# A gated attention and sign-weight FFN block on one core: row statistics taken a batch sooner, signs taken one by one, first weights' low parts split otherwise, raw output weights in another place

## The reference

```
xn  = layernorm(x)                       # per row, eps 1e-5
q   = xn @ wq.T ; k_new = xn @ wk.T ; v_new = xn @ wv.T
k   = concat(ctx, k_new) ; v = concat(ctx, v_new)     # 1024 keys
att = softmax(q @ k.T / sqrt(512)) @ v
x   = x + tanh(g_xattn) * (att @ wo.T)
h   = relu((layernorm(x) @ sign(up).T) * up_scale)    # 2048 hidden
x   = x + tanh(g_ffn) * (h @ sign(down).T) * down_scale * output_scale
```

## Time and profile before

| | |
|---|---|
| median of 3 runs | 663.87 us (663.48 to 664.93) |
| profiled execution's own time | 664.24 us |
| its span, first to last instruction | 662.5 us |
| TensorE busy | 602.3 us (91%) |
| VectorE busy | 382.2 us (58%) |
| ScalarE busy | 290.0 us (44%) |
| GpSimd busy | 132.7 us (20%) |
| mean granted TensorE clock | 0.964 |

### The profile page before, as it was taken

One profiled execution on the slowest core, in us unless ns is written; L12 is line 12 of the kernel. 1 busy time (PEld: TensorE's weight loads), 2 busy tenths in 40 slices (PEclk: granted clock), 3 DMA queues, 4 the chain that ended last, 5 costly groups with the idle time before them and its releaser, 6 DMA issues.

```text
span 662.5 us, 7100 instructions
## 1 busy us (share of the span) xinstructions
PE 602.3 (91%) x2738; PEld 494.3 (75%) x2738; DVE 382.2 (58%) x527; ACT 290.0 (44%) x426; POOL 132.7 (20%) x116
## 2 busy tenths in 40 slices
PE   7959993999993999994999986999999999999997
PEld 6747772888872888873888865888888787888885
DVE  4498724267734248744158753965555955666564
ACT  3573601154511146521137436546565834555541
POOL 5673000202000201100200300431423201324001
PEclk9969996999997999998899997999999999999999
DMA  8603202010201104101102013220101031132011
GB/s 290 234 0 129 64 0 77 19 63 1 64 1 34 62 17 174 64 1 32 63 1 95 2 63 127 72 88 33 63 33 64 32 128 32 54 107 96 1 64 63
DMA packets 20097, 43.21 MB, mean 65 GB/s; under 512 B 4832, under 2 KB 4832, under 8 KB 19680
## 3 DMA queue, kind: packets, MB, share of 16 engines
q1 hardware_dynamic: 20064, 42.76, 19.0%
HBM read 36.45 MB, written 6.30 MB: 65 GB/s over the span
## 4 chain that ended last, share of the span: by engine, by line
PE 68%; DMA 9%; issue 8%; DVE 8%; ACT 5%; POOL 2%; SPq 0%; POOLq 0%; DVEq 0%; ACTq 0%
PE proj L527 19%; PE score L657 17%; PE turn L642 11%; PE score L527 7%; DMA row_facts<-mean_rstd 4%; PE proj L642 4%; PE score L560 4%; PE proj L560 2%; DMA all_facts<-row_facts 2%; DVE raw_t L1200 2%; DMA raw_w<-in_ffn_w 1%; POOL four_x L455 1%; PE score L788 1%; DVE turned_x L1299 1%; DVE turned_x L1302 1%
## 5 line engine op out<-in xcount | busy, mean ns | idle before, releaser
L657 PE MATMUL score<-down_signs,hid_split 128*128 128x512 f32 x512 | 133.8, 390 | 0.6 <-DVE normed L1515 0.5
L527 PE MATMUL proj<-probsT,four_x 128*128 128x512 f32 x384 | 97.7, 416 | 35.2 <-DVE four_x L1179 35.2
L527 PEld LDWEIGHTS proj<-probsT,four_x 128*128 128x128 f32 x384 | 76.8, 203 | 53.9 <-DVE four_x L1179 37.5
L657 PEld LDWEIGHTS score<-down_signs,hid_split 128*128 128x128 f32 x512 | 95.8, 188 | 21.7 <-DVE hid_split L1482 0.9
L527 PE MATMUL proj<-four_x,weights 128*128 128x512 f32 x336 | 79.2, 396 | 5.8 <-ACT raw_q L888 5.8
L455 POOL TENSOR_TENSOR four_x<-raw_ctx,four_x 128x2048 fp32r<-128x2048 f32 x8 | 37.2, 4645 | 216.5 <-ACT four_x L869 216.5
L527 PEld LDWEIGHTS proj<-four_x,weights 128*128 128x128 f32 x336 | 64.2, 192 | 19.9 <-issue 6.6
L1179 DVE TENSOR_TENSOR four_x<-proj,four_x 128x512 fp32r<-128x512 f32 x32 | 22.0, 689 | 54.4 <-ACT four_x L877 54.4
L1482 DVE TENSOR_TENSOR hid_split<-hid,hid_split 128x512 fp32r<-128x512 f32 x64 | 44.0, 690 | 15.8 <-ACT hid_split L1093 15.6
L527 PE MATMUL proj<-weights,four_x 128*128 128x512 f32 x192 | 51.9, 405 | 0.0
L642 PE MATMUL turn<-ops_b,up_ops 128*128 128x512 f32 x192 | 51.8, 391 | 0.0
(11 more groups left out here) (128 smaller groups left out, 885.9 us busy)
## 6 DMA issues: line engine op xcount, KB each, us to landing
raw_w<-in_ffn_w SPq DMA_DIRECT2D x24, 512.0 KB, 3.3
raw_ctx<-in_ctx_turned SPq DMA_DIRECT2D x4, 1024.0 KB, 5.3
raw_ctx<-in_ctx SPq DMA_DIRECT2D x4, 1024.0 KB, 5.8
result<-rows SPq DMA_DIRECT2D x16, 256.0 KB, 2.0
rows<-in_x SPq DMA_DIRECT2D x3, 1024.0 KB, 5.4
turned_x<-in_x_turned SPq DMA_DIRECT2D x3, 1024.0 KB, 5.3
rows_away<-rows SPq DMA_DIRECT2D x1, 2048.0 KB, 10.8
rows<-rows_away SPq DMA_DIRECT2D x1, 2048.0 KB, 7.6
```

Source lines behind the costliest of these rows:

```text
L527: last = pe.matmul(bank, lhs(l), rhs(r), start=start and i == 0, stop=stop and i == 2)
L657: last = pe.matmul(wide(r), hid_split[:, n % HR, s, r * P:(r + 1) * P], down_signs[:, chunk_of(q), :], start=(q == 0 and s == HI), stop=(q ...
```

## The change

- `row_facts`/`all_facts` become a function of their own, `next_facts`. In batches 1 and 2 SP calls `next_facts(b+1)` ahead of `next_rows(b+1)`, right after the raw context of batch b. Row statistics of batch b + 2 are taken by VectorE after the attention of batch b is added, ahead of the next keys, and `inverse_std(b+1)` stands ahead of the value context's low part on GpSimd. Batch 1's statistics are still taken in batch 0, after the last probabilities.
- `norm_turned` stands behind `proj_out` of e = 0 (in batch 0: behind e = 3), `next_rows_low` behind e = 1 (3), and `next_hi` on ScalarE behind e = 1 (3).
- In the start, VectorE makes the low parts of `wq` and of the first turned context; GpSimd makes those of `wk` as before, then waits for batch 0's last score operand (S4) before those of `wv`, the value context and `wo`. The high parts of `wv` and `wo` move into batch 0. `t_high(T1)` moves behind key 2. There is one `w_ready` semaphore for each matrix.
- Raw `wo` lies in `rows[8:12]`, the place of `wq` and of batch 2's `x`, and is loaded after `wq` is split; batch 2's `x` is loaded after `wo` is split.
- The first attention product waits for the new values one row tile at a time.
- In the last batch the eight sign pieces are taken at different points of ScalarE's queue instead of four in a row.

```diff
-    SPLIT = {W_K: 0, W_Q: DC, W_O: 2 * DC, W_V: 3 * DC}
+    SPLIT = {W_K: 0, W_Q: DC, W_V: 2 * DC, W_O: 3 * DC}
-                  W_O: probs[:, 0:2, :].rearrange("p s (k n) -> p (s k) n", n=DIM)}
+                  W_O: rows[:, 2 * RT:3 * RT, :]}
@@ SP
-            sp.dma_start(raw_of[W_O], wo.rearrange(row_tiles, p=P)).then_inc(w_in[W_O], 16)
...
+            sp.wait_ge(w_ready[W_Q], DC)
+            sp.dma_start(raw_of[W_O], wo.rearrange(row_tiles, p=P)).then_inc(w_in[W_O], 16)
...
+                if b == 0:
+                    sp.wait_ge(w_ready[W_V], DC)
+                    sp.dma_start(rows[:, 3 * RT:4 * RT, :], x_v[3]).then_inc(x_in[3], 16)
+                    next_rows(1)
+                    next_facts(1)
+                    sp.wait_ge(w_ready[W_O], DC)
+                    sp.dma_start(rows[:, 2 * RT:3 * RT, :], x_v[2]).then_inc(x_in[2], 16)
+                elif b + 1 < BATCH:
+                    next_facts(b + 1)
+                    next_rows(b + 1)
@@ GpSimd
             weight_low(W_K, 3)
-            for i in range(DC):
-                weight_low(W_Q, i)
-            context_low(turned_split(0))
-            for i in range(DC):
-                weight_low(W_O, i)
-            for i in range(DC):
-                weight_low(W_V, i)
             for b in range(BATCH):
+                if b == 0:
+                    pool.wait_ge(s_ready, nth(S_LO, 0, S4))
+                    for i in range(DC):
+                        weight_low(W_V, i)
+                else:
+                    inverse_std(b + 1)
                 context_low(values_split(b))
-                inverse_std(b + 1)
+                if b == 0:
+                    for i in range(DC):
+                        weight_low(W_O, i)
+                    inverse_std(1)
@@ TensorE
-                pe.wait_ge(proj_lo, values_out(b, RT - 1))
...
+                        if e == 0:
+                            pe.wait_ge(proj_lo, values_out(b, i))
...
+                if b == 0:
+                    pe.wait_ge(w_ready[W_O], DC)
@@ ScalarE
-                if e == 1:
+                if e == 2:
                     t_high(b, T1)
...
+                if b == 0:
+                    for i in range(DC):
+                        weight_high(W_V, i)
...
                 context_high(values_split(b))
+                if last_batch:
+                    take_signs(0)
                 exponentials(b, 2)
+                if last_batch:
+                    take_signs(1)
                 exponentials(b, 3)
...
                 probs_out(b, 2)
+                if last_batch:
+                    take_signs(2)
...
                 proj_out(m + 2, new_side[:, HI, 2, :])
+                if last_batch:
+                    take_signs(3)
...
-                    for n in range(4):
-                        take_signs(n)
+                    take_signs(4)
                     two_rows_out(0)
-                    take_signs(4)
...
+                    if e == (3 if b == 0 else 1):
                         act.wait_ge(turned_normed, b + 1)
@@ VectorE
+                if b == 0:
+                    dve.wait_ge(x_in[1], 16)
+                    norm_stats(RT)
+                    norm_moments(1)
+                    means(1)
...
+                    for e in range(DC):
+                        proj_out(b, DC + e, chunk(qT, e))
+                        if e == (3 if b == 0 else 0):
+                            norm_turned(b + 1)
+                        if e == (3 if b == 0 else 1):
+                            next_rows_low(b + 1)
...
+                if b + 2 < BATCH:
+                    dve.wait_ge(x_in[b + 2], 16)
+                    norm_stats(RT * (b + 2))
+                    norm_moments(b + 2)
+                    means(b + 2)
...
-            keys(0)
+            first_weight_low(W_Q, 0)
+            first_weight_low(W_Q, 1)
+            t_sum(0, T1)
+            first_weight_low(W_Q, 2)
+            first_weight_low(W_Q, 3)
+            t_sum(0, T3)
+            t_sum(0, T2)
+            t_sum(0, T4)
+            dve.wait_ge(ctx_hi, turned_split(0) + 1)
+            dve.tensor_tensor(ctx_side[:, LO], raw_ctx[:, :, :], ctx_side[:, HI].bitcast(F32), ALU.subtract
+                              ).then_inc(ctx_ready, 1)
+            t_low(0, T3)
```

More of the change, by code:

```diff
@@ L213, in gated_block @@
         tanh_done, gain_done = sem("tanh_done"), sem("gain_done")
-        w_hi, w_ready = sem("w_hi"), sem("w_ready")
+        w_hi = sem("w_hi")
+        w_ready = {w: sem(f"w_ready{w}") for w in (W_K, W_Q, W_V, W_O)}
         first_rstd = sem("first_rstd")
@@ L358, in _ @@
             sp.dma_start(hid_gain[:, :], up_scale).then_inc(small_in, 16)
-            sp.wait_ge(w_ready, SPLIT[W_K] + DC)
+            sp.wait_ge(w_ready[W_K], DC)
             sp.dma_start(rows[:, RT:2 * RT, :], x_v[1]).then_inc(x_in[1], 16)
[L362 to L365, removed]
+            sp.wait_ge(w_ready[W_Q], DC)
+            sp.dma_start(raw_of[W_O], wo.rearrange(row_tiles, p=P)).then_inc(w_in[W_O], 16)
             def context_rows(b):
@@ L376, in next_rows, with next_facts @@
                 sp.dma_start(turned_x[:, :, :], x_turned_v[b]).then_inc(turned_x_in, 16)
+            def next_facts(b):
                 sp.wait_ge(rstd_done, b)
@@ L607, in v_jobs @@
                 if b == 0:
-                    pe.wait_ge(w_ready, SPLIT[W_V] + DC)
+                    pe.wait_ge(w_ready[W_V], DC)
                 for r in range(RT):
@@ L812, in _ @@
             for e in (0, 1):
-                pe.wait_ge(w_ready, e + 1)
+                pe.wait_ge(w_ready[W_K], e + 1)
                 first_k_half(e, 0, PASS[2])
@@ L829, in _ @@
             for e in range(DC):
-                pe.wait_ge(w_ready, SPLIT[W_Q] + e + 1)
+                pe.wait_ge(w_ready[W_Q], e + 1)
                 if e >= 2:
@@ L1039, in batch @@
                     return
+                if b == 0:
+                    act.wait_ge(small_in, 16 * 5)
+                    act.activation(gates[:, :], gates_raw[:, 0:2], ACT.Tanh).then_inc(tanh_done, 1)
+                    for i in range(DC):
+                        weight_high(W_O, i)
                 for e in range(DC):
                     proj_out(m + 4 + e, qT[:, HI, e, :])
-                    if e == 0:
+                    if e == (3 if b == 0 else 1):
                         act.wait_ge(turned_normed, b + 1)
@@ L1421, in batch @@
                 else:
-                    dve.wait_ge(x_in[b + 1], 16)
-                    norm_stats(next_tile0)
-                    norm_moments(b + 1)
-                    means(b + 1)
-                    proj_out(b, 4, chunk(qT, 0))
-                    norm_turned(b + 1)
-                    proj_out(b, 5, chunk(qT, 1))
-                    next_rows_low(b + 1)
-                    proj_out(b, 6, chunk(qT, 2))
-                    proj_out(b, 7, chunk(qT, 3))
+                    for e in range(DC):
+                        proj_out(b, DC + e, chunk(qT, e))
[3 more added lines that the diff above has]
+                            next_rows_low(b + 1)
                 if last_batch:
@@ L1449, in first_stats, with first_weight_low @@
                 dve.tensor_scalar(var_eps[:, r:r + 1], mean_var[:, r, 1:2], EPS, None, ALU.add).then_inc(eps_done, 1)
+            def first_weight_low(w, i):
+                dve.wait_ge(w_hi, SPLIT[w] + i + 1)
+                dve.tensor_tensor(weights[:, w, LO, i, :], raw_of[w][:, i, :], weights[:, w, HI, i, :].bitcast(F32),
+                                  ALU.subtract).then_inc(w_ready[w], 1)
             def first_norm(r):
```

31 lines of the change are left out of this document (7 added, 24 removed).

## The result

The changed kernel takes 599.3 us in the median of 4 runs (598.72 to 602.57), against 664.14 us for the kernel before, timed beside it: ratio 0.9033, 95% interval 0.8999 to 0.9068. The forecast was 601.0 in a range of 597 to 612. The profiled execution took 599.61 us with a span of 597.8, 64.7 less than before.

The account below looks back on a forecast made before the run. TensorE bounds the kernel, busy 91% of the span. Gains 12.2 + 12.3 + 27.3 + 11.0 = 62.8 cut span 662.5 to 599.7; with 1.74 around it 601.4, less 0.4 for the profiled execution 601.0; range 597 to 612.

Parts of the forecast that it names:

- Section 1: Start to batch 0's values: GpSimd silent, VectorE undisturbed, A11 at 35.1 instead of 44.99; gain 12.2 us.
- Section 2: Batch 0's values to batch 1's A11: work at full clock, less a new 2.0 us stop at K2; gain 12.3 us.
- The clock: Batch 0 to 1, behind the new stop: no clock loss taken; about 2 us worse if such a stop were enough.
- rival A: Small stops where covers are 0.5 to 2 us thick: 8 to 12 us, 609 to 613; chance 0.24 together with B.
- Section 3: Batches 1 and 2, A11 to A11: all work at full clock, 88.2 us each; gain 13.7 + 13.6, 27.3 us.
- Section 4: Last batch to first FFN group: waits of 0.97 and 7.67 and 2.4 of lower clock go; gain 11.0 us.
- Rivals B: Batch 0 to 1 stays as it was, inverse root waiting for wo: 607 to 613 us; chance 0.24 together with A.
- C: Batches 1 and 2: SP still gets to the store late, 24 to 27 us stay, 626; chance 0.05.
- D: Whole kernel slower than before: unbroken TensorE run gets less clock, 696 us at 0.85; chance 0.03.

Follow-up runs that it names:

- e1: Kernel before, only norm_turned and next_rows_low moved behind e = 3's proj_out in all three changes of batch; 634.7 us, ratio to before 0.9572.
- e6: Changed kernel with GpSimd again making the low parts of wq and of the first turned context, VectorE none; 604.46 us, ratio 0.9088.
- e7: Changed kernel without GpSimd's wait for S4 ahead of wv's low parts; 601.73 us, ratio 0.9058.
- e8: Changed kernel with key_out 0 and 1 of batch 1 ahead of the turned context's high part on ScalarE; 597.94 us, ratio 0.8996.
- e2: Changed kernel with statistics of batches 2 and 3 in the batch in front and normalization behind e = 3 everywhere; 603.15 us, ratio 0.9091.
- e10: Changed kernel with the 2 MB rows_away issued behind the store and load of batch 3's facts; 601.37 us, ratio 0.9042.
- e12: Changed kernel with t_high(T1) behind key 1 in ScalarE's queue instead of behind key 2; 603.81 us, ratio 0.9073.
- e3: Changed kernel with statistics of batches 2 and 3 in the batch in front, normalization at the change's own early place; 620.86 us, ratio 0.9361.
- e5: Changed kernel with the old single wait for all four row tiles of new values ahead of the attention; 604.26 us.
- e4: Changed kernel with sign pieces 0 to 3 in a row after the last probabilities, as before; 610.64 us.
- e11: Changed kernel with key_out 0 and 1 ahead of context's high part, inverse_std(1) ahead of wo's low parts, norm_turned(1) behind e = 2; 597.45 us, ratio 0.8983.

## Why the prediction was right

- **Section 1 (12.2, came 13.1).** The forward timeline had A11 at 35.1; it came at 34.47. TensorE was 0.4 us earlier than in the kernel before already at Q0 (23.56 against 23.96); e1, with the old start, has Q0 at 23.34, so that part is scatter and luck. The mechanism is confirmed by e6 and e7: T3 took 1.23 us here. How the gain splits between the engines is known for 3.9 us of it only.
- **Section 2 (12.3, came 12.5).** The new stop was put at K2, behind `key_out(0)`, with 2.0 us; it was there with 1.62 of idle, 1.94 in all. The facts were at hand when `norm_turned` started at 91.36 (forecast 92.3), `next_lo` at 100.24 (101.3). e8 shows the cause. In the traces of e2, e6, e7, e8, e10 and e12 the same facts came 0.2 to 1.9 us too late for `norm_turned`. So the stop is not a fixed number: over the traces that keep this order it is 1.35 us (e3) to 2.04 (e12), and K0 stops too in three of them (0.37 in e2 and e7, 1.32 in e12).
- **The clock.** I took no cost for this stop. In the profiled execution there is none: 72 products in 16.64 us. In e6 and e7 there is, see below, and this is the part of rival A that was real. That it cost nothing in the profiled execution is partly luck. One of the four executions took 602.57 and has no trace; its mean granted clock is 0.997 against 0.998, and 0.001 of 600 us is 0.6 (1.2 at most, by the rounding). So the clock explains a part of its 3 us at most, and the rest stays open; facts that land later, as above, are a candidate. The Trainium skill (TensorE: Matmul & The Clock Gate, Why this matters for your kernels) warns of idle gaps between bursts of matmuls. The traces agree for 1.87 us in e6 and 1.98 in e7, and show no loss behind 1.87 in e10 and 2.04 in e12.
- **Section 3 (27.3, came 27.8).** The sum is right. What it does not say is that two edits can each buy most of it. With the place behind e = 3 and no sooner statistics, e2 keeps 24 us of it (2.5 of them, by e5, from the wait for the values, the rest mostly from the place); the last 4 need the early place, and by e3 that place costs 21.6 unless the statistics are taken a batch sooner. Two margins were off: the inverse root of batch 2 was done at 114.4, 51 us before its use and not some 60, and batch 3's facts landed some 25 us before theirs and not 16.
- **Section 4 (11.0, came 11.3).** The stop and its clock went, and no sign piece stood in the way of the probabilities. e4 gives it back.
- **An edit costed at nothing** was worth something: `t_high(T1)` behind key 2. I had seen that T1 "may be held to 114.5" (it was held 4.69 us, to 113.25), and had not asked what stood behind its high part on ScalarE in the old order. e1 paid for that three times, and e12 shows its price in the changed kernel: 1.10 at Q0 and 1.13 at A11. The change had the right order, and the forecast didn't know why: that is luck.
- **Rivals B, C and D** did not occur. `wo`'s low parts took 5.05 us undisturbed, the store in batch 1 was issued at 119.02 and its facts were used at 165.04, and the granted clock was 1.00 from 20 us to 597, with 571.3 of 577 us busy, twice as long as before (1.00 from 413.6 to the end). The Trainium skill (DMA: Bandwidth & Descriptors, Queues, rings and completion order) has each DMA engine consume its descriptors in ring order. e10 agrees in direction; measured it is 3.7 us.

## What to carry to other kernels

When an engine waits for a DMA, look at what stands behind that wait in its queue before you try to make the DMA earlier: three edited lines gave 29 us of 65. Making the data come earlier is worth most where the use has to stand early; here it gave the last 4 us, by making the early place free. Build the timeline forward, engine by engine, to the next instruction that would be late; in this case it named the place of the one new stop, and its length to 0.4 us. Don't read a stop's price off its idle time alone: here it was some 0.3 more each time. And remove a small stop even if it seems to cost little: e11 gained 1.9 us from one of 1.6, and its executions scatter less (0.43 us against 3.85), though the runs don't show what all of the scatter was.

## What the runs showed of the hardware

- A stop of some 1.9 us, with TensorE at full clock ahead of it, cost 1.6 us more in clock in two traces, and nothing in others. Behind 1.62, 1.68 and 1.83 us 72 products took 16.6 us; behind 1.87 us they took 16.61 in e10 and 18.23 in e6, and behind 1.98 us 18.25 in e7. Behind 2.04 us in e12 24 products took 5.73, the time at full clock. So the length of the stop alone doesn't decide, and what does is not shown. The rows of e7, e10 and e12:

```profile
110.88 18.25 PE L539 MATMUL proj<-four_x,weights 128*128 128x512 f32 x72 [1.98 <-ACT raw_new L898]
```

```profile
107.82 16.61 PE L540 MATMUL proj<-four_x,weights 128*128 128x512 f32 x72 [1.87 <-ACT raw_new L899]
```

```profile
111.54 5.73 PE L540 MATMUL proj<-four_x,weights 128*128 128x512 f32 x24 [2.04 <-ACT raw_new L899]
```

The window view of e6 behind that stop has the granted clock at 0.53 (columns as in the earlier trace rows):

```profile
112.10:115.00 2.90, 2.84 (x7) 2.26 (x8) 2.30 (x1) 0.50 (x2) 2.90 (x1) 0.53 0.00 0
```

- The 4-KB store of 1024 single 4-byte values to HBM took, over all traces and from its issue to that of the load that waits for it, 8.3 to 11.9 us with no large transfer issued just ahead, 12.6 to 14.4 right behind 1 MB, 16.8 to 18.4 behind 3 MB. In the order of batches it took 11.03, 10.37 and 8.37 before, and about the same in e1, e2 and e3; why the last is faster was not tried.
- In these traces GpSimd and VectorE hold each other up for whole instructions when VectorE reads two SBUF operands. T1 in the changed kernel started 1.0 us behind the start of GpSimd's 4.61-us instruction and took 4.69 instead of 1.22, to 1.08 us behind that instruction's end; GpSimd's next one, 0.20 us elsewhere, took 1.19. With one operand in PSUM VectorE kept its 0.68 (e7).
